# Two edits to a decoder kernel: a local transformer with paired score steps and one merged feed-forward stage, and a state-space recurrence with squares and scaling on ScalarE

## The reference, cut to what matters

```python
# layer 1: six rounds; 16 heads of 64, windows of 32 queries that see 64 keys
for i in range(6):
    x = attn_layer(shift_tokens(x), Wqkv[i], ...) + x   # q, k: l2norm, scale, rotary; softmax; @ Wo
    x = ffn_layer(shift_tokens(x), ...) + x             # layer norm; a * gelu(gate) with 341 inner columns; @ W2
# layer 2: a recurrence over the tokens t, state h of 256 channels x 16 per batch
h = h * dA_t + dB_t * x_t[:, :, None]
nrm = sqrt(sum(h * h));  fac = minimum(20.0 / (nrm + 1e-08), 1.0)
h = where(t % 10 == 0, h * fac, h)                      # at every tenth token
y = einsum('bdn,bn->bd', h, C_t) + D_param * x_t
```

## Time and profile before

| | us |
|---|---|
| median of three timed runs | 6191.43 (6186.78 to 6191.97) |
| the profiled execution | 6185.92 |
| its span in the profile | 6184.0 |
| PE busy, share of the span | 5032.6, 81% |
| DVE busy | 3189.3, 52% |
| ACT busy | 2957.8, 48% |
| POOL busy | 1901.8, 31% |

### The profile page before, as it was taken

One profiled execution on the slowest core, in us unless ns is written; L12 is line 12 of the kernel. 1 busy time (PEld: TensorE's weight loads), 2 busy tenths in 40 slices (PEclk: granted clock), 3 DMA queues, 4 the chain that ended last, 5 costly groups with the idle time before them and its releaser, 6 DMA issues. The chain is left out here.

```text
span 6184.0 us, 108311 instructions
## 1 busy us (share of the span) xinstructions
PE 5032.6 (81%) x39346; PEld 3240.5 (52%) x39346; DVE 3189.3 (52%) x6332; ACT 2957.8 (48%) x8829; POOL 1901.8 (31%) x2082
## 2 busy tenths in 40 slices
PE   3998598978878878878788788778989944787888
PEld 2664255756636546546456456458886632223433
DVE  5551354556546446455356366358875544562433
ACT  2442244547647657556467477355534412352421
POOL 0230000347637457367277187001112300000000
PEclk6999799999989989899899799776669966895888
DMA  1000000001101111111111011000000000000000
GB/s 48 2 1 4 19 10 16 1 14 39 47 19 41 40 29 36 35 34 35 31 39 41 25 40 41 32 1 1 1 1 5 1 3 4 10 4 29 4 0 7
DMA packets 34520, 122.70 MB, mean 20 GB/s; under 512 B 8484, under 2 KB 9512, under 8 KB 32424
## 3 DMA queue, kind: packets, MB, share of 16 engines
q1 hardware_dynamic: 33960, 115.42, 6.9%
HBM read 36.43 MB, written 1.05 MB: 6 GB/s over the span
## 5 line engine op out<-in xcount | busy, mean ns | idle before, releaser
L640 POOL MEMSET norm_eps<- 128x1 f32 x16 | 1.6, 99 | 1905.7 <-POOLq L116 1847.2
L2087 POOL TENSOR_TENSOR local_rot<-local_raw,local_cos 128x512 f32<-128x512 f32 x384 | 488.1, 1271 | 303.5 <-DVE local_raw L2131 303.5
L2090 POOL TENSOR_TENSOR local_other<-local_raw,local_sin 128x256 f32<-128x256 f32 x768 | 557.6, 726 | 60.2
L2029 ACT ACTIVATE ps<-ps,local_negmax 128x96 f32<-128x96 f32 x1536 | 489.2, 322 | 37.2 <-DVE local_negmax L2110 36.9
L1952 PE MATMUL ps<-arena,local_xs 128*128 128x512 f32 x768 | 447.4, 667 | 71.8 <-ACT local_xs L2009 52.0
L2093 POOL TENSOR_TENSOR local_rot<-local_rot,local_other 128x512 f32<-128x512 f32 x384 | 487.4, 1269 | 30.1
L2024 ACT ACTIVATE local_squares<-ps 128x512 f32<-128x512 f32 x384 | 230.8, 601 | 508.2 <-PE ps L1952 507.8
L2117 DVE TENSOR_REDUCE local_norm<-local_squares 128x8 f32<-128x512 f32 x384 | 263.2, 685 | 282.4 <-ACT local_squares L2024 282.4
L1940 PE MATMUL ps<-local_K,local_Q 64*64 64x96 f32 x6144 | 337.0, 249 | 0.0
L2029 ACT ACTIVATION_READ_ACCUMULATOR ps<-ps,local_negmax 128x1 f32 x1536 | 331.0, 215 | 0.0
L2519 PE MATMUL ps<-ssm_BC,const 32*128 32x40 f32 (+1 forms) x3584 | 297.8, 373 | 26.4 <-PEq L116 22.0
(11 more groups left out here) (499 smaller groups left out, 11465.9 us busy)
## 6 DMA issues: line engine op xcount, KB each, us to landing
local_V_span<-local_V SPq DMA_DIRECT2D x96, 384.0 KB, 4.0
local_V_span<-local_V SPq DMA_DIRECT2D x96, 256.0 KB, 3.5
arena<-in_L1f_a SPq DMA_DIRECT2D x7, 2176.0 KB, 8.2
local_V_span<-local_V SPq DMA_DIRECT2D x72, 128.0 KB, 2.3
arena<-in_L3f SPq DMA_DIRECT2D x1, 3460.0 KB, 11.6
arena<-in_L1f_f SPq DMA_DIRECT2D x6, 537.5 KB, 4.0
arena<-in_L0f SPq DMA_DIRECT2D x1, 2824.5 KB, 9.8
arena<-in_L0x SPq DMA_DIRECT2D x1, 2049.5 KB, 9.0
```

Source lines behind the costliest of these rows:

```text
L2029: nc.scalar.activation(scores, scores, ACT.Exp, bias=m.negmax[:, s % 2, u:u + 1], accum_out=m.total[:, s % 2, u:u + 1])\
L2087: link(nc.gpsimd.tensor_tensor(rot, raw, m.cos[:, t, a * DH:(a + 1) * DH].unsqueeze(1) .broadcast_to([P, 8, DH]), ALU.mult))
L2090: link(nc.gpsimd.tensor_tensor(other[:, :, lo:lo + HALF], raw[:, :, HALF - lo:DH - lo], m.sin[:, t, a * DH + lo:a * DH + lo + HALF].unsque ...
```

## The change

Attention. The lead is 7 steps. V is made in the first two steps of each tile's four instead of the second and third, five steps ahead. TensorE does the q or k product first, and then, in even steps alone, the scores of two steps, interleaved so that the four products of a unit (two heads, two steps) go to the four 64x64 quarters of the array, in two banks. VectorE takes over the copies of V and of the heads' output from ScalarE; the floor of the norm becomes a bias of the log and a minimum inside the scaling.

Feed-forward. One stage for all four batches: means, variances and inverse deviations (log and exp, no square root) pipelined over the batches, then 12 pieces of gate and linear products, each output product one piece later, residuals at the end of each batch.

Recurrence. Squares and the scaling of the ends go to ScalarE (four multiplications per segment, one per batch). VectorE forms `pre`, the product of the next rates with the unscaled ends, before the factor is known, and multiplies it by the factor. ScalarE's decays are made in quarters, B and C are spread over all four segments of a chunk, and y is summed per segment: 2 x 16 products with 40 moving columns.

```diff
 # local_attention, TensorE
-                if 0 <= s < G:
-                    tile, half_span, half = place(s)
-                    pe.wait_ge(flip_read, flips_until(4 * tile + 2 * half + 1))
-                    if s >= 3:
-                        pe.wait_ge(probs_ready, s - 2)
...
+                if 0 <= s < G and s % 2 == 0:
+                    tile, half_span, _ = place(s)
+                    pe.wait_ge(flip_read, 4 * tile + 2 * 1 + 2)
+                    if s >= 2:
+                        pe.wait_ge(probs_ready, s - 1)
...
+                    for i in range(2):
+                        nc.tensor.matmul(SC[(s + i) % 3][:, 0:UNITS * SPAN], m.unit[:, :],
+                                         m.bands[:, edge, :, :].rearrange("p u k -> p (u k)"), start=True, stop=False)
+                    for u in range(UNITS):
+                        for h in range(2):
+                            for i in range(2):
+                                c = UNITS * i + u
+                                rows = slice(DH * h, DH * h + DH)
+                                mm = nc.tensor.matmul(SC[(s + i) % 3][rows_of(h, i), u * SPAN:(u + 1) * SPAN],
...
 # local_attention, VectorE, after the row maxima of step s
+                    nc.vector.scalar_tensor_tensor(out=heads(m.raw[:, n % 4, :]),
+                                                   in0=m.inverse[:, n % 4, :].unsqueeze(2).broadcast_to([P, 8, DH]),
+                                                   scalar=1e12, in1=heads(bank("qk", n)[:, :]), op0=ALU.min, op1=ALU.mult)\
+                      .then_inc(scaled, 1)
...
+                    nc.vector.tensor_copy(m.V[:, tile % 2, i * 512:(i + 1) * 512], bank("v", v)[:, :]).then_inc(v_read, 1)
...
+                    nc.vector.tensor_copy(m.oT[:, tile % 2, :, SPAN_Q * half_span:SPAN_Q * (half_span + 1)],
+                                          OUT[:, :].rearrange("p (c q) -> p c q", q=SPAN_Q)).then_inc(out_read, 1)
 # gelu_ffn, TensorE
+            for k in range(B + 2):
+                if k < B:
...
+                    nc.tensor.matmul(MEAN[k % 2][:, :], core.average, m.xs[:, k, :], start=True, stop=True)\
+                      .then_inc(mean_ready, 1)
...
+            for q in range(B * M + 1):
+                if q <= LAST:
...
+                    for i, name in enumerate(("W1_gate", "W1_lin")):
+                        mm = nc.tensor.matmul(core.ps[2 * (q % 3) + i][0:rows[k], :],
+                                              w(name, k * P, k * P + rows[k]), normal[:, b, :], start=True, stop=True)
...
+                    mm = nc.tensor.matmul(OUT[b % 2][:, :], w("W2", k * P, (k + 1) * P)[0:rows[k], :], hidden(q - 1),
+                                          start=(k == 0), stop=(k == M - 1))
 # state_recurrence, TensorE
-                    if exists(k - 1) and i < 2:
...
-                        for n in range(SSM_N):
-                            mm = nc.tensor.matmul(y_rows(k - 1, i), core.ident,
-                                                  H[:, (k - 1) % 2, 0:segs_of[k - 1], :, i * SSM_N + n, :]
-                                                  .rearrange("p s b t -> p b s t"),
-                                                  start=(n == 0), stop=(n == SSM_N - 1))
...
+                    if r is not None:
+                        pe.wait_ge(weighed, 2 * (r + 1))
...
+                        for c in range(2):
+                            for n in range(SSM_N):
+                                mm = nc.tensor.matmul(y_rows(kk, c)[:, :, ii * SEG:(ii + 1) * SEG], core.ident,
+                                                      H[:, kk % 2, ii, :, c * SSM_N + n, :],
+                                                      start=(n == 0), stop=(n == SSM_N - 1))
+                            mm.then_inc(y_ready, 1)
 # state_recurrence, ScalarE
+                        nc.scalar.activation(sq[:, :, :], ends(k, i), ACT.Square, scale=1.0 / LIMIT).then_inc(sq_ready, 1)
...
+                            nc.scalar.mul(ends(k, i)[:, b, :], ends(k, i)[:, b, :], fac[:, b:b + 1]).then_inc(scaled, 1)
 # state_recurrence, VectorE
+                            link(nc.vector.tensor_tensor(pre[:, :, :], first[:, nk % 2, ni, :, :], ends(k, i), ALU.mult))
...
+                            link(nc.vector.tensor_tensor(scratch[:, :, :], pre[:, :, :], fac[:, :].unsqueeze(2)
+                                                         .broadcast_to([P, B, DN]), ALU.mult))
```

More of the change, by code:

```diff
@@ L1861, in local_attention @@
             uses.append(("qk", n))
[L1862 to L1865, removed]
+        if values_at(s) is not None:
+            uses.append(("v", 2 * values_at(s)[0] + values_at(s)[1]))
+        if turning_out(s) is not None:
+            uses.append(("out", turning_out(s)))
     use_at = {u: k for k, u in enumerate(uses)}
@@ L1954, in _ @@
                       .then_inc(qk_ready, 1)
+                if 0 <= s < G and s % 2 == 0:
[3 more added lines that the diff above has]
+                        pe.wait_ge(probs_ready, s - 1)
+                    first = tile % QT * TILE + SPAN_Q * half_span
+                    edge = int(tile % QT == 0 and half_span == 0)
+                    for i in range(2):
[7 more added lines that the diff above has]
+                                mm = nc.tensor.matmul(SC[(s + i) % 3][rows_of(h, i), u * SPAN:(u + 1) * SPAN],
+                                                      m.Q[rows, tile % 2, c, SPAN_Q * half_span:SPAN_Q * (half_span + 1)],
+                                                      m.K[rows, c, first:first + SPAN], start=False,
+                                                      stop=(u == UNITS - 1))
+                    mm.then_inc(scores_ready, 1)
+                n = s + LEAD - TURN_LAG
+                if 0 <= n < G:
+                    pe.wait_ge(rotated, n + 1)
+                    if n >= 1:
+                        pe.wait_ge(flip_read, n)
+                    for c in range(4):
+                        mm = nc.tensor.transpose(TURN[:, c * P:(c + 1) * P], m.rot[:, n % 4, c * P:(c + 1) * P],
+                                                 core.ident)
+                    mm.then_inc(flipped, 1)
+                if values_at(s) is not None:
+                    tile, i = values_at(s)
+                    v = 2 * tile + i
+                    wait_for_bank("v", v)
+                    nc.tensor.matmul(bank("v", v)[:, :], tokens_of(tile),
+                                     w("Wqkv", (4 + i) * 512, (5 + i) * 512), start=True, stop=True)\
+                      .then_inc(v_ready, 1)
                 g = s - 1
@@ L1962, in _ @@
                     mm.then_inc(turned, 1)
[L1963 to L1979, removed]
                 g = s - 2
```

496 lines of the change are left out of this document (309 added, 187 removed).

## The result

The changed kernel takes 6848.3 us (median of 4 runs, 6774.77 to 6852.44) against 6189.1 (6184.11 to 6191.97): ratio 1.1038, 95% interval 1.101 to 1.1066. I had forecast 6257 and at most 6330. The sign was right, and for the reason given, the recurrence; the size was wrong by 590 us.

What follows compares the result with a forecast made beforehand. PE was taken to pace attention, POOL close behind; nothing was full in feed-forward; PE and DVE were nearly full in the recurrence. 6185.9 - 262 - 218 + 548 = 6254, forecast as 6257 us, range 6180 to 6330.

Steps and rivals of the forecast that it cites:

- Moved copies: Attention: 64 copies a round leave ACT, as many reach DVE; ACT 198 us, DVE at most 248, below POOL's 268.
- The 1.32 wait goes: Attention: PE's 1.32 us wait before the output projection disappears, its bank being released a step earlier.
- serial loop of some 3.8 us: Attention: ACT and DVE's loop per step (squares, sum, maxima, four exps, copy) takes some 3.8 us, below 4.2.
- rival (2): Attention: scores run two at a time or in-order loops miss each other; 308 us a round, total 6319; chance 0.18.
- four quarters: Attention: four array quarters run at once, 32 score instructions taking what 16 did; gain 0.9 us per pair.
- The floor by POOL: Attention: POOL's unchanged rotations, 64 x 4.19 us, plus lead and tail make a round at least 295.0 us.
- The 298: Attention: forecast us per round, above the floor of 295.0 for occasional misses and a longer lead; gain 262 over six rounds.
- 58.7 us: Feed-forward: forecast time per round against 95.0, a gain of 218 us over six rounds.
- the price of a sum: Recurrence: each 40-column y instruction costs 0.2135 us at half clock, 64 per segment making 13.7 us.
- the clock of 0.50: Recurrence: PE stays at half clock over the whole stage, giving 1087 us, a loss of 548.
- the spreading: Recurrence: 64 spreading instructions per segment at 0.089 us each at half clock, 5.7 us.
- The lower bound of 525: Recurrence: smallest loss in us expected at half clock, with no switches and a norm product of 0.5.

Runs made afterwards that it cites:

- e_oT_dve_first: Changed kernel with the recurrence of before and the output copy kept on VectorE but first in its step; 5811.4 us, ratio 0.9353.
- e_oT_act: Changed kernel with the recurrence of before and the output copy back on ScalarE, first in its step; 5810.5 us, ratio 0.9382.
- e_F: Kernel before with only the merged feed-forward of the change; 6011.8 us, ratio 0.9707.
- e_y_once: Changed kernel with y summed once per chunk, 160 columns an instruction; 6307.3 us, ratio 1.0167.
- e_fill4: Changed kernel with four unused 384-column products a segment added ahead of the norm's product in the recurrence; 6904.0 us, ratio 1.1169.
- e_dve_sq: e_oT_act with a recurrence keeping quartered decays, early start values and VectorE's new order; y, spreading as before, squares and scaling on VectorE; 5824.1 us, ratio 0.9422.
- e_oT_mid: Changed kernel with the recurrence of before and the output copy on VectorE between the scaling and the value copy; 5967.9 us, ratio 0.97.
- e_two_quarters: e_oT_act with the second step's scores sent to the same partition halves as the first's; 5869.6 us, ratio 0.9524.
- e_fill: Changed kernel with one unused 384-column product a segment added ahead of the norm's product in the recurrence; 6902.3 us, ratio 1.118.
- e_sq_only: e_dve_sq with the recurrence's squares on ScalarE, the scaling still on VectorE; 5838.6 us, ratio 0.9412.
- e_y_two: Changed kernel with y summed for two segments at a time, 80 columns an instruction; 6502.7 us, ratio 1.0479.
- e_half_rot: e_oT_act with one sine product of GpSimd's rotation and half of its sum left out, for timing alone; 5765.7 us, ratio 0.9292.
- e_AF: Changed kernel with the recurrence of before, so attention and feed-forward new; 6228.8 us, ratio 1.004.

## Why the prediction was wrong, by its own steps

**The step that failed** is in the attention part: "Moved copies", costed as load (DVE at most 248 us a round, below POOL's 268), and "The 1.32 wait goes, since the bank before the projection is now released a step earlier". Both look at how much each engine does and not at what stands behind what. In place of a gain of 262 us came a loss of 231. The output copy left the head of ScalarE's step for a place on VectorE behind an operation that waits for ScalarE, which waits for VectorE, which waits for ScalarE's squares of PE's product in the same step. With the heads product waiting for the copy, PE's next product stands behind that, and the loop closes once a step pair: QK product, squares, norm, log, exp, scaling, value copy, output copy, heads product. My "serial loop of some 3.8 us" had squares, sum, maxima, exps and one copy, and left out the log, the scaling and the two copies that close this circle. The loads themselves did no harm, as e_oT_dve_first shows: VectorE is busy 206.7 us a round, ScalarE 218.5 (I had 198), both below GpSimd's 255.5. Here the 1.32 wait became 1.90 and 2.16, two waits a tile; over the span it is 338.6 us, 56 a round, and the falling clock adds some 30. That e_oT_dve_first takes it all back shows the copy's place in the step, not its engine, to be the cause; with the copy in its old place the attention is what rival (2) had, 308.

**The terms around it.** PE's work of the attention was right: four quarters (0.89 us), and the tile's 16.5 us; e_oT_act needs 274.7 a round, 17.2 with fill and drain. The floor by POOL was right in kind: in e_oT_act's first round the rotations start from 1356.54 to 1627.55, 271.0 / 63 = 4.30 us each against 4.19. The 298 was 11 too low, as rival (2) had it ("the in-order loops miss each other").

**Feed-forward.** Forecast 58.7 us from last addition to next first work; measured 55 to 59, PEclk 0.93. Right, with a gain of 238 for 218.

**Recurrence.** The mechanism and the price of a sum were right, as was the clock of 0.50 and the forecast that PE's load, not VectorE's relief, decides. Two terms were too small: the spreading, 332.4 + 25.6 us in 3584 instructions, is 0.100 and not 0.089 each (I had divided a run of 128; a run of 64 takes 6.23, 0.097, and 96 take 8.82), +40 us; and the waits ahead of y, 32.0 us by its group, where I had taken a switch or two. With y and the norm's products 6 and 5 us above their terms, and less what the groups overlap (1130.8 us by group, 1118.0 of PE busy), these are the 65 us missed. The lower bound of 525 doesn't follow from its own terms either: 22 + 52 x 19.9 + 14.2 = 1071 is a loss of 532.

**The narrow stage** was in no step. Its 61 us are clock, not work, and hit e_F as well, which has neither the new attention nor the new recurrence.

**The rules weighed there.** The Trainium skill's "TensorEngine Tiling (Array Packing)", section Instruction Overhead, puts about 60 cycles on each matmul. The trace of before had already shown another price for this shape, and the runs agree with its rows: 0.215 us at 40 and 0.218 at 80 columns. The Trainium skill's "TensorE: Matmul & The Clock Gate", section HAM oscillation, describes a loop in which a wait of 3 to 5 us for DMA makes the engine start cold again each time. The attention's rows show the same kind of fall (0.10 busy, then 0.50) behind a wait for another engine, with pauses of about 2 us and not after each of them. The same page of the Trainium skill, section The HAM clock gate, lets activity release the throttle; the recurrence differs, since PE was busy 10.00 of 10.00 us at 0.50 in the earlier trace rows and 1118 of 1152.5 after, and only longer streams raised it: y of 160 columns (mean 0.61 in e_y_once) and e_fill4's four products (0.62).

## What to carry to other kernels

When an operation is moved to another engine, ask first what it will stand behind there and who waits for it, and follow that chain until it closes; the sum of busy times can't see a loop. On PE, count instructions before columns when the weights are 128 wide and the moving side is 80 columns or less; that is shown here for f32 at a clock of 0.50. A short pause of PE in a tight loop costs itself and, when the clock falls, the slow stretch behind it: in the attention these were about equal halves.

## What was unexpected of the hardware

An unchanged stage of 1208 PE instructions takes 220 to 283.5 us, at a granted clock of 0.75 or 0.54, from one kernel's profile to another's, whatever the change: 1% of the total, more than the 0.2% that I had taken. Single runs of one kernel lie as far apart (e_dve_sq: 5756.85 to 5835.06 us); that this stage is what tells them apart is likely and not shown, as each kernel has one profile. The profiles speak for it: at the short end of their kernel's times (e_dve_sq, e_oT_mid, e_two_quarters, e_fill) the stage takes 220 to 226 us, at the long end (e_sq_only, e_y_two, e_half_rot) 284; e_AF, at the short end with 247, fits less well. The kernel before, timed 13 times beside e_AF, has such a spread too, 6170.39 to 6234.52 us. And more work can be nearly free: 318 long products beside e_fill's 106, 171 us of PE, came with a stage that was 18 us shorter.
